# Eighteen projection pieces of an image in another order: values, queries, keys

## The reference, cut to what matters

```
def proj(W, b):
    return (x @ W + b).reshape(B, L, H, D).transpose(0, 2, 1, 3)
Q, K, V = (proj(Wq, bq), proj(Wk, bk), proj(Wv, bv))
...
s_rest = jnp.einsum('bhld,bhlwd->bhlw', Q[:, :, 1:], Kw) * scale
...
a_rest = jax.nn.softmax(s_rest, axis=-1)
out_rest = jnp.einsum('bhlw,bhlwd->bhld', a_rest, Vw)
```

## Time and profile before

| what | value |
|---|---|
| median of 3 runs | 3102.83 us (3099.03 to 3105.12) |
| profiled execution, its own time | 3101.95 us |
| span of the profiled execution, first to last instruction | 3100.2 us |
| PE busy | 2628.2 us, 85% of the span |
| DVE busy | 1836.3 us, 59% |
| ACT busy | 1124.6 us, 36% |
| POOL busy | 815.0 us, 26% |
| granted clock of PE, mean | 0.93 of full speed |

### The profile page before, as it was taken

One profiled execution on the slowest core, in us unless ns is written; L12 is line 12 of the kernel. 1 busy time (PEld: TensorE's weight loads), 2 busy tenths in 40 slices (PEclk: granted clock), 3 DMA queues, 4 the chain that ended last, 5 costly groups with the idle time before them and its releaser, 6 DMA issues.

```text
span 3100.2 us, 49397 instructions
## 1 busy us (share of the span) xinstructions
PE 2628.2 (85%) x17619; PEld 1919.8 (62%) x17619; DVE 1836.3 (59%) x5182; ACT 1124.6 (36%) x3347; POOL 815.0 (26%) x656
## 2 busy tenths in 40 slices
PE   1359797999898999999898999999998989998397
PEld 0237575767676676667676666767576766766264
DVE  4345464656666565656666665756666666656354
ACT  0024243434343434434343434334343434343122
POOL 0000021223232322223232312232232322232344
PEclk9769788999999999998999999999989999999699
DMA  2430011324224242324333242423242241414464
GB/s 39 92 116 14 23 53 26 93 65 103 67 60 110 35 115 49 91 66 103 71 83 85 40 128 30 118 54 94 65 103 65 50 122 23 126 36 136 117 152 101
DMA packets 272628, 241.72 MB, mean 78 GB/s; under 512 B 209020, under 2 KB 250494, under 8 KB 261760
## 3 DMA queue, kind: packets, MB, share of 16 engines
q1 hardware_dynamic: 211648, 147.17, 17.8%
q0 software_dynamic: 50880, 52.59, 10.3%
q10 hardware_dynamic: 9856, 38.80, 3.9%
HBM read 133.29 MB, written 73.59 MB: 67 GB/s over the span
## 4 chain that ended last, share of the span: by engine, by line
PE 67%; DVE 19%; ACT 4%; issue 4%; DMA 1%; POOL 1%; SPq 1%; ACTq 0%; DVEq 0%; POOLq 0%
PE PSUM L1532 10%; PE PSUM L1509 9%; PE PSUM L1580 7%; PE PSUM L1602 5%; PE PSUM L1550 4%; PE PSUM L1518 3%; PE PSUM L1552 3%; PE PSUM L1551 3%; DVE HLO L1057 3%; PE PSUM L1448 3%; PE PSUM L1404 2%; PE PSUM L1592 2%; DVE HHI L1054 2%; PE PSUM L1445 2%; PE PSUM L1677 2%
## 5 line engine op out<-in xcount | busy, mean ns | idle before, releaser
L1532 PE MATMUL PSUM<-XT,WB 128*128 128x512 f16 x2010 | 522.8, 393 | 46.9 <-DMA META<-slots 43.5
L702 POOL DMA_INDIRECT out_dram<-Y,META x228 | 363.5, 1594 | 643.9 <-DVE Y L1081 517.6
L842 ACT ACTIVATE PSPT<-PSUM,NMX 94x126 f32<-94x126 f32 x1056 | 367.1, 358 | 370.8 <-PE PSUM L1592 188.0
L810 ACT ACTIVATE HF<-PSUM,WB 128x512 f32<-128x512 f32 x402 | 273.9, 685 | 526.6 <-PE PSUM L1532 525.7
L1550 PE MATMUL PSUM<-WB,HHI 128*128 128x192 f16 x1608 | 400.8, 249 | 48.7 <-DVE HLO L1057 47.5
L1551 PE MATMUL PSUM<-WB,HHI 128*128 128x192 f16 x1608 | 399.1, 248 | 0.0
L1552 PE MATMUL PSUM<-WB,HLO 128*128 128x192 f16 x1608 | 399.0, 248 | 0.0
L1054 DVE TENSOR_SCALAR HHI<-HF 128x512 f16<-128x512 f32 x402 | 172.3, 429 | 354.2 <-ACT HF L810 351.8
L1532 PEld LDWEIGHTS PSUM<-XT,WB 128*128 128x128 f16 x2010 | 197.3, 101 | 227.2 <-issue 47.1
L1580 PE MATMUL PSUM<-KBD,QT 128*94 128x378 f32 x704 | 308.4, 522 | 9.7 <-ACT PSPT L842 8.1
L1057 DVE SCALAR_TENSOR_TENSOR HLO<-HF,HHI 128x512 f16<-128x512 f32 x402 | 278.3, 692 | 13.8
(11 more groups left out here) (270 smaller groups left out, 4542.6 us busy)
## 6 DMA issues: line engine op xcount, KB each, us to landing
WB<-weights SPq DMA_DIRECT2D x67, 1600.0 KB, 6.9
XR<-in_x ACTq DMA_DIRECT2D x16, 768.0 KB, 5.2
out_dram<-X ACTq DMA_DIRECT2D x32, 384.0 KB, 3.0
weights<-WB ACTq DMA_DIRECT2D x4, 1600.0 KB, 6.1
GUP<-TGU SPq DMA_DIRECT2D x256, 8.0 KB, 1.8
slots<-XROW,IDX POOLq DMA_INDIRECT x256
out_dram<-Y,META POOLq DMA_INDIRECT x228, 3.6
HF<-in_w ACTq DMA_DIRECT2D x6, 384.0 KB, 4.6
```

The source lines that it names most:

```text
L702: pool.indirect_dma_start(out[:, :], bass.IndirectOffsetOnAxis(row, 0), Y[:, wslot(i, j), q, :], None, bounds_check=B * T + BS - 1, oob_is ...
L810: act.activation(HF[:, k % 2, :], PSUM[:, 4 + k % 2, :], ACT.Gelu, scale=1 / (X_UP * W_UP), bias=bias).then_inc(f["gelu_done"], 1)
L842: e = act.activation(PS[0:QS, n % 2, h, :], PSUM[0:QS, n % 2, h * KS:(h + 1) * KS], ACT.Exp, bias=NMX[:, b, n % 2, h:h + 1], accum_out=DEN ...
L1532: mm = pe.matmul(dst, WB[:, ws, w:w + 128], XT[:, xs, chunk, :], start=(n == 0), stop=(n == 4))
```

## The change

A list ORDER gives, for each place 0 to 17, which piece stands there: first the six value pieces, then the six of queries, then the six of keys. PSUM bank, engine and waits go by the place, the contents by the piece. Since six is even, every piece stays on the engine that it had.

```diff
--- before.py
+++ after.py
@@ -495,12 +495,14 @@
 
         SPANS = [(0, 4), (4, 8), (8, NB)]
         PIECES = 18
+        ORDER = [12, 13, 14, 15, 16, 17] + list(range(12))
         act_engine = nc.scalar
 
         def evacuate_piece(eng, n, give):
 
             src = bank(n % 4)
             is_act = eng is act_engine
+            n = ORDER[n]
             if n < 6:
                 oh, (b0, b1) = n // 3, SPANS[n % 3]
                 k = b1 - b0
@@ -1500,22 +1502,23 @@
                     m = n - 4
                     nm = ("piece_act", "piece_dve")[m % 2]
                     pe.wait_ge(s[nm], at(nm, i, m // 2 + 1))
+                place, n = n % 4, ORDER[n]
                 if n < 12:
                     W = WQ if n < 6 else WK
                     oh, (b0, b1) = (n % 6) // 3, SPANS[n % 3]
                     keys = slice(PAD, PAD + QB) if n < 6 else slice(0, KS)
                     width = (b1 - b0) * (QB if n < 6 else KS)
                     for j in range(2):
-                        mm = pe.matmul(PSUM[0:HC, n % 4, 0:width], W[:, j, oh * HC:(oh + 1) * HC],
+                        mm = pe.matmul(PSUM[0:HC, place, 0:width], W[:, j, oh * HC:(oh + 1) * HC],
                                        XW[:, j, b0:b1, keys], start=(j == 0), stop=(j == 1))
                     if n < 6 and n % 3 == 2:
                         for j in range(2):
-                            mm = pe.matmul(PSUM[0:HC, n % 4, 400:401], W[:, j, oh * HC:(oh + 1) * HC],
+                            mm = pe.matmul(PSUM[0:HC, place, 400:401], W[:, j, oh * HC:(oh + 1) * HC],
                                            XW[:, j, 0, KW:KS], start=(j == 0), stop=(j == 1))
                 else:
                     for b in range(2 * (n - 12), min(2 * (n - 12) + 2, NB)):
                         for j in range(2):
-                            mm = pe.matmul(PSUM[0:KS, n % 4, (b % 2) * C:(b % 2 + 1) * C], XW[:, j, b, :],
+                            mm = pe.matmul(PSUM[0:KS, place, (b % 2) * C:(b % 2 + 1) * C], XW[:, j, b, :],
                                            WV[:, j, :], start=(j == 0), stop=(j == 1))
                 mm.then_inc(s["piece_done"], 1)
```

## The result

The changed kernel took 3131.53 us (median of 4 runs, 3128.04 to 3136.99); the kernel before took 3102.5 beside it (4 runs, 3099.03 to 3105.12). The ratio is 1.0096, 95% interval 1.0078 to 1.0114: slower by 24 to 35 us. The forecast was 3141.7, range 3120 to 3160. What was measured is the case that I had given 27%, the sum without the clock term (3131.6), and not the one that I had given 52%.

The account below looks back on a forecast made before the run. PE's standing still was taken to bound the kernel. 3101.95 us plus 25.2 (end, thirteen images), 4.4 (three images alone) and 10.1 (clock falls) gave 3141.7 us, range 3120 to 3160.

Parts of the forecast that it names:

- the one that I had given 52%: The forecast itself: both end costs plus falls of PE's clock in six of thirteen images, 3141.7 us.
- What bounds, and where: PE's standing still bounds; its only stream gap, 0.80 us ahead of the last ffn2, grows; start and middle cost 0.
- The price at the end, 13 x 1.94: Stream's end in thirteen images: key copies delay the last ffn2 and first score, net 1.94 us each, 25.2 us.
- The three images alone, 3 x 1.48: Images whose pieces lie among no chunks: DVE's last copy takes 1.84 instead of 0.36 us, 4.4 us in all.
- The clock, +10.1: PE's granted clock falls after the longer end waits in six of thirteen images, 1.69 us each: 10.1 us.
- 20 us gained and 14 lost: Bounds if existing clock falls move: eleven middle images all as fast as 170.72 us, or as slow as 173.77.
- No fall: Rival: the new waits at the stream's end bring no clock fall, only the end costs, 3131.6 us; 27%.
- A fall in each: Rival: PE's clock falls after the end waits in every one of thirteen images, 3153.6 us; 14%.
- Hidden: Rival: the last two ffn2 cover the key copies, only the three images alone pay, 3106.4 us; 4%.
- eaten: Rival: PE's 43.5 us wait behind the last image, for rows of tokens, absorbs the lateness, 3102 us; 3%.

Follow-up runs that it names:

- e1: Changed order, but the last two value pieces stay at places 16 and 17: 3114.5 us, 1.0047 of the kernel before.
- e2: Order of the kernel before, only its last two key pieces moved behind the values to places 16 and 17: 3131.9 us, 1.0103 of the kernel before.
- e3: Kernel before with only ACT's last piece, at place 16, one of keys; DVE's last stays a value piece: 3144.9 us, 1.0140 of the kernel before.
- e6: Kernel before in its old order, ACT's copy of place 16 put behind the last gelu: 3113.7 us, 1.0023 of the kernel before.
- e5: Changed kernel, ACT's copy of place 16 put behind the last gelu: 3118.1 us, 1.0053 of the kernel before.
- e11: Changed kernel with spare matmuls on PE in five waits that each image had all along: 3093.1 us, 0.9999 of the kernel before.
- e8: Changed kernel with ten spare matmuls on PE in the new wait between the last two ffn2: 3121.7 us, 1.0075 of the kernel before.

## Why the prediction was right, and which term was not

*What bounds, and where: right.* PE's only gap at the end of the stream grew, the pieces in front of it cost PE next to nothing (e1, 0.14 us an image), and the two last places hold the whole cost (e2).

*The price at the end, 13 x 1.94: right*, each instant to 0.01 us and 1.98 us in all, because the kernel before held the same neighbours on ACT and DVE six places earlier, where their lateness was hidden. e3 to e6 show which of them: ACT's three copies ahead of the gelu; put behind the gelu, the loss in the distance to the score goes and more (e5).

*The three images alone, 3 x 1.48: right*, 2.02 for 0.54.

*The clock, +10.1: the mis-sized term.* I took the rate of falls, six in thirteen, from another wait, and their price, 1.69 us, from one attention. In the changed kernel's profile one attention in thirteen had its fall behind the new wait, and over the runs the rest was 218 us before and after: the net term was 0. That is luck as much as reason, since the falls did not stay as they were. They became fewer behind the first score (three to one) and more ahead of the pieces (six to ten). Nor was 1.69 the price: the image with the fall takes 178.87, 4.8 us more than the others, and its later falls differ from theirs.

Nor is 0 a property of this wait. Behind the same 1.87 us the clock fell in eight of thirteen attentions of e11, and behind e3's 2.48 us in all. The step that failed was to treat falls as chances of a single wait. e1 shows that they are not: the same work and nearly the same waits in another order, and the rest is 13 us higher. That it matters when, along the whole image, the waits come fits this, but no run tests it alone. I had set 20 us gained and 14 lost as bounds for falls that move elsewhere; over e1 to e8 the rest went from 13 us below to 30 above the kernel before, so the bound on the losing side was too narrow. The shortest of the eleven images takes 170.67, not 170.72, which changes neither.

*The rivals.* "No fall" was the right one in its sum, 3131.6, though one image had a fall. "A fall in each" is out by the other twelve. "Hidden" fell by the timeline, "eaten" by the wait of 43.5 us, as long as before.

*Open.* Why the images of the changed kernel settled at 174.1 us, with a fall ahead of the pieces in ten of thirteen and hardly one behind the new wait, while e11's have none ahead of the pieces and eight behind the wait. A version with a fixed delay at the start, to shift all images alike, wasn't tried.

## What to carry to other kernels

The end of a software pipeline has no next stage to hide behind: put last the pieces with the shortest copies, and let no copy stand ahead of the activation that feeds the last matmuls. (Here the second gave its gain in time only where PE's other waits were filled, or the keys stood last.) A price can often be read off the same instructions elsewhere in the old trace. Before crediting a gain or a loss of one per cent to an edit, split each run into span times mean clock and the rest; here the first moved within some 10 us of what was worked out, except where spare matmuls were added, and the second by as much as the gains and losses themselves. Instants in the trace between which the clock is full are surer than either.

## What the runs showed of the hardware

- Span times one minus the granted clock was 218 of 3100 us in the kernel before. It is an upper bound for what the lower clock cost: 45 of it lie in the first 213.8 us, in which PE worked for 59. Spare matmuls in five waits of 0.7 to 2.2 us per image brought it to 135: 65 us less time (3100.5 to 3035.5) for work that computes nothing.
- Kernels whose first score comes at instants almost 3 us apart (changed, e5, e6) had ten, seven and four of eleven images within 0.2 us of 174.1, those of e5 and e6 at a mean clock of 0.94 for 0.96: a gain of PE came back as a lower clock. This was seen, not explained.
- After a short wait the clock can stay low for long: two attentions of e11 ran at a mean of 0.53 for 17.3 us with PE without a gap.
